# Later wide weights, w_hyper pieces from another queue, and a drain in pairs: a four-layer conditioned block on one core

## The reference

```
# 1  attention (16 heads of 16) and a gated network, both with conditioned norms
x = x + a_alpha * attention(gamma * rmsnorm(x) + beta)
x = x + f_alpha * (silu(h @ gate_w.T) * (h @ hidden_w.T) @ out_w.T + out_b)
# 2  gelu network, its activation rounded to 8 bits per token, its weight to -1, 0, 1
u = (x * scale * rsqrt(mean(x*x) + eps)) @ up_w.T ; val, gate = split(u)
h = round8(val * gelu(gate)) ; x = x + h @ ternary(down_w).T
# 3  adapter whose two matrices are computed from the condition (w_hyper, 16.8 MB)
down = relu(x @ (Wd + 0.1 * dWd).T + bd) ; x = x + down @ (Wu + 0.1 * dWu).T + bu
# 4  layer norm with a conditioned offset
x = ((x - mean) * rsqrt(var + eps) * w + b + tanh(cond @ lin_w.T + lin_b)) * w + b
```

## Time and profile before

| | us |
|---|---|
| median of 3 runs | 1007.7 |
| lowest, highest | 1006.65, 1009.4 |
| the profiled execution | 1011.21 |
| its span | 1009.4 |
| TensorE busy in it | 954.4 (95%) |
| VectorE, ScalarE, GpSimd busy | 742.5, 567.4, 230.6 |

### The profile page before, as it was taken

One profiled execution on the slowest core, in us unless ns is written; L12 is line 12 of the kernel. 1 busy time (PEld: TensorE's weight loads), 2 busy tenths in 40 slices (PEclk: granted clock), 3 DMA queues, 4 the chain that ended last, 5 costly groups with the idle time before them and its releaser, 6 DMA issues.

```text
span 1009.4 us, 20749 instructions
## 1 busy us (share of the span) xinstructions
PE 954.4 (95%) x6530; PEld 781.5 (77%) x6530; DVE 742.5 (74%) x1718; ACT 567.4 (56%) x1169; POOL 230.6 (23%) x303
## 2 busy tenths in 40 slices
PE   5678899999999999999999999999999999998995
PEld 4345569788887979788888979787888879796873
DVE  3844458787878888787878887887878787886645
ACT  2264564756656574756565564746566565746442
POOL 1412602122121312121221313121221213121320
PEclk9788899999999999999999999999999999999997
DMA  8787742040404022130404031130404031220000
GB/s 275 246 281 268 280 153 76 26 123 3 147 1 130 17 83 64 43 104 1 147 1 139 8 101 47 53 93 16 131 1 147 1 121 27 73 65 2 22 22 10
DMA packets 76271, 89.42 MB, mean 89 GB/s; under 512 B 16512, under 2 KB 62864, under 8 KB 73616
## 3 DMA queue, kind: packets, MB, share of 16 engines
q1 hardware_dynamic: 70160, 63.07, 20.7%
q0 software_dynamic: 2304, 16.78, 4.7%
q10 hardware_dynamic: 3776, 9.18, 2.4%
HBM read 63.14 MB, written 25.31 MB: 88 GB/s over the span
## 4 chain that ended last, share of the span: by engine, by line
PE 84%; DVE 4%; issue 4%; DMA 4%; ACT 2%; POOL 1%; SPq 0%; ACTq 0%; DVEq 0%; POOLq 0%
PE bank L706 17%; PE bank L770 15%; PE bank L720 8%; PE bank L665 7%; PE bank L675 6%; PE bank L620 6%; PE bank L647 6%; DMA hyper<-w_hyper 3%; PE bank L683 3%; PE bank L629 3%; PE bank L787 3%; PE bank L599 2%; PE bank L807 2%; PE bank L780 1%; PE bank L801 1%
## 5 line engine op out<-in xcount | busy, mean ns | idle before, releaser
L526 POOL TENSOR_TENSOR act_lo<-act_f,act_hi 128x256 fp32r<-128x256 f32 x120 | 88.3, 736 | 364.7 <-ACT act_hi L1129 364.7
L1398 DVE TENSOR_REDUCE neg_max<-bank 128x2 f32<-128x512 f32 x256 | 162.1, 683 | 0.1
L1086 ACT ACTIVATE probs<-bank 128x512 f32<-128x512 f32 x256 | 134.5, 601 | 26.5 <-PE bank L665 13.7
L1165 ACT ACTIVATE gelu_g<-bank,r 128x256 f32<-128x256 f32 x128 | 60.7, 474 | 93.8 <-PE bank L770 92.4
L706 PE MATMUL bank<-h_hi,gh_hi 128*128 128x256 f32 x512 | 103.5, 284 | 2.8 <-DVE h_lo L1461 2.8
L1123 ACT ACTIVATE silu_g<-bank 128x256 f32<-128x256 f32 x128 | 49.1, 383 | 98.9 <-PE bank L706 98.4
L706 PE MATMUL bank<-h_lo,gh_hi 128*128 128x256 f32 x512 | 103.2, 283 | 0.0
L706 PE MATMUL bank<-h_hi,gh_lo 128*128 128x256 f32 x512 | 102.9, 283 | 0.0
L1467 DVE TENSOR_TENSOR act_f<-bank,silu_g 128x256 f32<-128x256 f32 x128 | 53.8, 420 | 63.1 <-ACT silu_g L1123 63.1
L1129 ACT ACTIVATE act_hi<-act_f 128x256 fp32r<-128x256 f32 x128 | 53.4, 417 | 75.3 <-DVE act_f L1467 73.0
L706 PEld LDWEIGHTS bank<-h_hi,gh_hi 128*128 128x128 f32 x512 | 82.8, 189 | 12.6 <-issue 7.8
(11 more groups left out here) (203 smaller groups left out, 2010.0 us busy)
## 6 DMA issues: line engine op xcount, KB each, us to landing
hyper<-w_hyper POOLq DMA_DIRECT2D x16, 1024.0 KB, 6.6
q_stack<-q_dram SPq DMA_DIRECT2D x96, 128.0 KB
k_stack<-k_dram SPq DMA_DIRECT2D x96, 128.0 KB
q_dram<-probs SPq DMA_DIRECT2D x16, 512.0 KB, 2.8
k_dram<-probs SPq DMA_DIRECT2D x16, 512.0 KB, 2.8
x_res<-xT SPq DMA_DIRECT2D x16, 256.0 KB, 2.9
delta_dram<-hyper_s ACTq DMA_DIRECT2D x15, 256.0 KB, 3.2
out<-xc SPq DMA_DIRECT2D x15, 256.0 KB, 2.5
```

The lines of the kernel that those rows point to most:

```text
L526: pool.tensor_tensor(act_lo[:, c % 3, :], act_f[:, c % 2, :], act_hi[:, c % 3, :].bitcast(F32), ALU.subtract).then_inc(g_lo.sem, 1)
L1086: act.activation(probs[:, h % SLOTS], halves(SCORE_BANKS[h]), ACT.Exp, scale=float(H / D) ** 0.5).then_inc(s_exp.sem, 1)
L1165: act.activation(gelu_g[:, n % 2, :], halves(7 - n % 2)[:, 1, :], ACT.Gelu, scale=r3[:, t:t + 1])\
L1398: dve.tensor_reduce(neg_max[:, qt, :, pair:pair + 1].rearrange("p a o -> p (a o)"), halves(n % 3), AX_X, ALU.max, negate=True).then_inc(ma ...
```

## The change

Prologue: the first quarter of w_cond is a load of its own, the rest follows behind w_qkv and x of batch 1, which goes to the idle tile x1. VectorE's norm of batch 0 stands ahead of its wait for the products, batch 1's norm ahead of the table of conditions. Products that nothing reads (`keep_busy`) stand before and behind the first ones. The first k stack goes by GpSimd's queue, with a semaphore of its own. The loads of raw weights 0 and 1, of w_down and of the first w_hyper pieces now wait for the first stack; q and k of batch 1 are written ahead of w_down. The reduction of w_down and the product over it move into run(0), behind the row maxima; VectorE copies the high part of raw weight 1. Low parts 0 and 1 on GpSimd stand behind the loads up to piece 5.

Pieces 8 to 15 of w_hyper are issued by SyncE, and products 0 to 5 and 6 to 15 stand at other places. VectorE scales pieces 2, 12 and 13.

Drain: adapter steps of batch 14 move one chunk earlier, its centre and variance ahead of batch 15's norm; the maximum over 1024 is taken per up chunk of 256, and the first half's quantising one chunk earlier; the tail's two halves go side by side, with `unread` products between; VectorE does one half of the output.

More of the change, by code:

```diff
@@ L292, in hyper_store, with stack_k @@
                 .then_inc(hyper_out[n % 4].sem, 16)
+        def stack_k(eng, count):
+            for a in range(2):
+                even = slice(64 * a, 64 * a + 32, 2)
+                odd = slice(64 * a + 1, 64 * a + 32, 2)
+                third = slice(64 * a + 32, 64 * a + 64, 2)
+                for rows_at, part in ((even, 0), (odd, 0), (third, 1)):
+                    src = k_dram[:, part].rearrange("(m a r) n -> a r m n", a=2, r=DH)[a]
+                    to = k_stack[rows_at].rearrange("r (m a) n -> r a m n", a=2)[:, a]
+                    eng.dma_start(to.bitcast(F32), src).then_inc(count.sem, 16)
         def whole(eng, run, drain):
@@ L465, in _ @@
                 sp.dma_start(w_o[:], w_oT.rearrange("(c p) n -> p c n", p=P)).then_inc(wo_in.sem, 16)
-                sp.wait_ge(n1_dve.sem, n1_dve.at(Batch(0)))
-                for c in range(DC):
-                    sp.dma_start(x_in[:, c, :], rows(batch_of(xT, Batch(1)))[:, c, :]).then_inc(x_in_dma.sem, 16)
                 sp.wait_ge(init_dma.sem, 32)
@@ L535, in run @@
                         low_part(4)
-                        pool.wait_ge(max_dma.sem, max_dma.at(a))
-                        for n in range(13, NHY):
-                            hyper_load(n)
                     if g:
@@ L1024, in _ @@
                 project_v(Batch(0), 1)
+                norm_a(Batch(1))
+                pe.wait_ge(cond_late.sem, 16)
                 cond_products(range(2, 8), bank[5])
-                norm_a(Batch(1))
                 project_qk(Batch(1), second=True)
-                pe.wait_ge(table.sem, TABLE - 1)
-                pe.wait_ge(ternary.sem, 1)
-                pe.matmul(bank[5][:, 0:1], ones[:], w_abs, start=True, stop=True).then_inc(abs_mm.sem, 1)
                 whole(pe, run, drain)
```

259 lines of the change are left out of this document (146 added, 113 removed).

## The result

The changed kernel took 1006.87 us (median of 16 runs, 1003.73 to 1010.31), the kernel before 1007.81 beside it (16 runs, 1006.40 to 1009.49). The ratio on record is 0.9976, 95% interval 0.9965 to 0.9987: about 2.4 us gained. It is not the quotient of the two medians, which are only 0.9 apart (0.9991, outside that interval); in the repeat, *after_again*, the ratio gives 2.6 and the medians 3.2. So the gain is real and small, some 1 to 3.5 us. The forecast was 997.5, its range 986 to 1002. It asked for 10.2.

A forecast was written before the change was run, and what follows sets the result against it. TensorE was busy 95% of the span, so gains were sought in waits at the two ends: 3.1 − 8.1 − 1.0 − 4.2 = −10.2 from the median 1007.7 gave 997.5 us, 8-in-10 range 986 to 1002.

The forecast's parts named there:

- Place 1: Start to the first batch's first normalisation: that would start at 65.3 instead of 62.20, +3.1 us.
- so w_down lands at about 45: Prologue loads: 6.3 MB at 375 GB/s take 17 us, so w_down lands at about 45, the row of maxima at 46.
- The mechanism with VectorE: Prologue: a VectorE ternary step beside GpSimd's low parts waits through all eight GpSimd steps, to 59.5; ternary steps end at 65.3.
- VectorE gets its turns: Rival on the prologue: VectorE gets turns or GpSimd comes late, place 1 gives −6.0 instead of +3.1, 988.4 us; chance 0.26.
- Place 2: w_hyper pieces beside batch 0's gates: SyncE's loads and later products remove 6.7 of waits and half-clock losses, −8.1 us.
- The megabytes are the bound: Rival: the same 37 MB pass in either order and the ends meet again, 1006 to 1009 us; chance 0.03.
- The pieces are late from SyncE too: Rival on the w_hyper pieces: place 2 gives −3.4, half its waits, instead of −8.1, 1002.2 us; chance 0.12.
- Place 3: The drain: −1.0 us up to the third up chunk and −4.2 behind the up stage.
- the third 1.0 earlier: Drain: the third up chunk, held by the table load and first gelu, starts 1.0 us earlier; bounds 0 and −2.

The follow-up runs named there:

- after_again: The changed kernel once more, nothing edited: 1006.25 us (11 runs), ratio 0.9974 to the kernel before.
- down_early: The changed kernel with the w_down load issued where it was before, ahead of ident and the vectors: ratio 0.9923 to the kernel before.
- mended: Changed kernel, w_down early, low parts held, SyncE's table-write wait moved to its first reader, ten unread products before the last projection: 998.41 us, ratio 0.9908.
- down_and_low: The changed kernel with w_down issued early and GpSimd's low parts held until VectorE's ternary steps end: ratio 0.9921 to the kernel before.
- low_later: The changed kernel with GpSimd's low parts 0 and 1 waiting until VectorE's ternary steps have ended: ratio 0.9916 to the kernel before (6 runs).
- pieces_pool: The changed kernel with loads of w_hyper pieces 8 to 15 issued by GpSimd again: ratio 0.9998 to the kernel before.
- old_prologue: The kernel before with the new drain and new schedule of w_hyper pieces 6 to 15, everything up to the first gates as before: 1001.36 us, ratio 0.9923.
- no_unread: The changed kernel without the tail's 22 products that nothing reads: ratio 0.9994 to the kernel before.
- before_again: The kernel before, nothing edited, traced once more: one execution, 1007.65 us, span 1005.8, no ratio.
- new_drain: The kernel before with the new drain alone, prologue and w_hyper pieces as before: 1005.55 us, ratio 0.9957.

## Why the prediction was wrong

The forecast was 3.1 − 8.1 − 1.0 − 4.2 = −10.2. By the ratios the three parts, each the difference of two, are: prologue +5.1 (0.9923 to 0.9974), pieces −3.4 (0.9957 to 0.9923), drain −4.3 (0.9957). Their intervals, from those of the two ratios, are ±2.8, ±2.7 and ±1.6: the signs are shown, the sizes only roughly. They add to −2.6, but that is no check, since such differences always add to the last ratio.

The traces give a second account, from means of the table: first gate +6.4 (81.3 in the four traces with the old prologue, 87.7 in the five with the unrepaired new one, without overlap), first to second gate stage −5.7 (74.0 and 68.3), the loop +0.8, the tail −3.6; together −2.1. The two disagree on how to share the loss between places 1 and 2, because these act on each other. What holds in both is the sum of the two: forecast −5.0, measured +1.7 or +0.7. That is the main error, about 6 of the 8 us.

**Place 1, forecast +3.1, measured +5 to +6.** Up to the maxima the steps held within 2 us: 10.64, 22.49, and maxima from 29.75 where 27.8 was said. Batch 1's projection took 5.90 at half clock and not 3.72 (I had argued that TensorE had no holes); that is the 2, and q and k of batch 1, and w_down behind them, left SyncE that much later. What failed is the step "so w_down lands at about 45, and the row of maxima, queued behind it and x_res, at 46". I counted megabytes and did not cost the small write at all. w_down landed at 48.4. The row was held by SyncE's wait for the table's write, 13.0 long, left at 45.84 and landed by 50.2. The scores began at 51.3 instead of 47.7. down_early shows that w_down alone was not it (scores at 50.3), mended that the write's wait was part of it (47.6, against 51.1 in down_and_low). The Trainium skill ("DMA: Bandwidth & Descriptors", Queues, rings and completion order) says that an engine goes round its queues packet by packet; 144 KB in 14.6 beside 1 MB in 17.6 are in line with that. But the small write also landed just behind the 512 KB k write ahead of it on its own queue, and no run separates the loads beside it from the write in front of it.

The mechanism with VectorE was right: the cast and twelve steps from 51.96 to 67.81, 15.9; with GpSimd idle 51.38 to 58.4, 7.0. Taking it away gave some 6 us at the end (low_later), moving w_down some 5 (down_early), and both together no more than either. Its form in the changed kernel was not quite as I put it. The cast itself was blocked through four GpSimd steps, and the ternary steps then went in turns, one per GpSimd step (1.39 beside 1.43). In down_early and pieces_pool it was as I put it: one ternary step waited through all eight (10.53 and 11.04). The Trainium skill ("SBUF — State Buffer", Who interferes with whom) has the pair held for one whole instruction, which gives VectorE its turn after each; the turns of 1.39 agree with it, 6.52 beside four steps and 10.53 beside eight do not. What decides between the two forms is open. The rival *VectorE gets its turns* needed that these turns were short enough to cost nothing, and is wrong: the first normalisation starts at 67.8, not 56.

**Place 2, forecast −8.1, measured −3.4 behind the old prologue.** In the pair of traces it came out almost exactly, 75.7 to 67.5, by luck, and it is wrong in two ways. The base was one execution, the longest of its kind: three traces with the old schedule have 75.7, 73.8 and 72.5, and their waits for pieces 6.7, 5.6 and 5.5, while I took 6.7 and two half-clock pairs from the first. And what the stage gives depends on the prologue: with the same new schedule it takes 72.0 from 79.0 on behind the old one and 67.5 to 68.7 from 86.5 to 89.2 on in the changed kernel. Pieces are waited for 2.6 and 3.4 where the first gate stands at 79.0 and 79.7 (old_prologue, mended), and 1.0 to 1.5 in the eight other traces with the whole new schedule, from 81.8 on; that fits loads that go on meanwhile. It is not all: mended, from 79.7 on, takes 69.7 and not 72.0, in part since it waits for the row of maxima 0.7 and not 2.2, and beyond 81.8 a later start shortens the stage hardly further (67.7 to 70.1 up to 83.9, 67.5 to 68.7 from 86.5 on). So the terms of places 1 and 2 were not independent, and I had added them. Up to the second gate stage the traces with the old pieces and prologue stand at 158.2, 153.2 and 156.5, mean 156.0, and the changed kernel's two at 154.0 and 157.6, mean 155.8. The rival *The megabytes are the bound* (0.03) named this outcome, 1006 to 1009, but not its reason: old_prologue and the repaired kernels move the same bytes and stand there at 149.3 to 152.6. The rival *The pieces are late from SyncE too*, which gave place 2 −3.4, has the right size for it, within ±2.7: in old_prologue pieces were waited for 2.6, and the row of maxima behind them in the queue 2.2.

**Place 3, forecast −1.0 and −4.2, measured −4.3 in all (±1.6, so −5.2 is not excluded).** Behind the up stage it is right: from the end of the last up product to the end of the span 23.9 and 23.5 before, 19.6 in both traces after. The shorter maxima, the side-by-side outputs and the held clock did what was said; the clock's part is 1.3 (no_unread). Ahead of it nothing was gained: from the last gate stage to the end of up took 41.0 and 39.9 before, 41.0 and 41.0 after. The third up chunk starts 32.4 behind the last gate stage in both first traces (973.96 here), and 31.5 behind it in before_again, where no half-clock stretch lies between. The second did come 1.0 earlier (29.9 against 31.0; before_again 30.0). The chain that the third waits for:

```profile
972.04 0.84 DVE r L1546
972.98 0.48 ACT gelu_g L1226
973.48 0.43 DVE act_u L1561
973.96 4.41 PE bank L804 x18
```

The step that failed is "the third 1.0 earlier". The mean and the guess of batch 14 went ahead, but VectorE does centre and layer_norm of batch 14 before the Newton step that gives r, and without r there is no gelu; TensorE waits 0.8 for act_u there. That r was late for this reason is read from the order of the steps, no run took it apart.

**Not in the sum:** the half-clock stretch before the drain, 1.2 or more where it occurs (before_again has one too; in the means it is the +0.8 of the loop). I had costed the stage between the two ends at nothing.

**The base.** I subtracted differences against a profile 3.5 above its own median from that median. before_again shows the excess to sit in the places that I was costing: the second gate stage 5.0 earlier and the tail 1.4 shorter there, with 2.9 lost in the loop. new_drain's trace, 156.5 at the second gate stage, shows that before_again is low in its turn.

## What to carry to other kernels

A wait read from one profile is a sample; before its removal is priced, compare the execution's own time with the median, and where it stands above all of them, take the waits as upper bounds. Count each wait of the queue that issues loads, also the one on a small write: behind a megabyte of writes and beside megabyte loads 144 KB took 14.6 us. Do not put VectorE's SBUF-to-SBUF copies and GpSimd's steps side by side on a path; do not add the gains of two stages that share one stream of loads; and judge a repair by the end and not by the first milestone that it moves: 3.5 us at the scores were 0.2 one stage later.

## What was not expected of the hardware

- A 144 KB write took 2.5 to 3.1 us in four traces with the old prologue and 13.3 to 14.8 in the ten with the new one, where a megabyte of writes stood just ahead of it on its queue and 1 MB loads were in flight; w_down, 1 MB, took 15.6 to 17.7 there in six traces and 5.4 to 6.2 in the eight where it was issued early.
- A cast of 128x2048 from float32 took 1.32 on VectorE alone and 6.52 beside four GpSimd steps of 1.25. Steps of 512 columns took 0.43 alone and 1.39 in turns with GpSimd's, and in two traces one of them took 10.53 and 11.04, through eight GpSimd steps. The steps that read a bank (0.48) kept their length beside GpSimd in low_later.
- Behind a wait of 2.5 to 2.6 us of TensorE the granted clock fell to half (1.2 of 2.4 GHz) in seven traces of seven with the new prologue, for 3.4 us in six and some 7 in one, and in one of four with the old, at the same instruction. Ten products ahead of it, 0.24 each, kept it at full clock in three traces of three.
